# Output bias moved to another place in GpSimd's queue, the maxima transposed ahead of the values, and the fourth head group's products laced into the subtraction

## The reference, cut to what matters

```
x = x + xattn(layernorm(x), ctx, Wq, bq, Wk, bk, Wv, bv, Wo, bo)
        q = (layernorm(x) @ Wq.T + bq) / 4,  k = ctx @ Wk.T + bk,  v = ctx @ Wv.T + bv   (16 heads of 16)
        softmax(q k^T, axis=-1) @ v, heads side by side, then @ Wo.T + bo
x = x + ffn(layernorm(x))
        e = argmax(xf @ router_w.T + router_b)            (32 experts, each token takes one)
        relu(relu(xf @ w1[e] + b1[e]) @ w2[e] + b2[e])
```

## Time and profile before

| what | value |
|---|---|
| median of three runs | 1201.5 us |
| the profiled execution, whole / its span | 1201.21 us / 1199.4 us |
| TensorE busy (matmuls) over the span | 1067.1 us, 89% |
| VectorE busy | 959.8 us, 80% |
| GpSimd busy | 852.9 us, 71% |
| ScalarE busy | 831.7 us, 69% |
| mean granted TensorE clock | 0.970 |
| attention stage | to about 945 us |

### The profile page before, as it was taken

The page is one execution under the profiler, slowest core; times in us unless marked ns, Lnnn a source line. Parts: engine busy times, 40 slices in busy tenths (PEclk is TensorE's granted clock), DMA queues, the critical chain, the costliest instruction groups (busy, mean ns, idle before and its releaser), DMA issues.

```text
span 1199.4 us, 38973 instructions
## 1 busy us (share of the span) xinstructions
PE 1067.1 (89%) x15015; PEld 889.2 (74%) x15015; DVE 959.8 (80%) x2321; ACT 831.7 (69%) x1892; POOL 852.9 (71%) x1613
## 2 busy tenths in 40 slices
PE   6999999899999999999999999999998429989893
PEld 4787777787777777777777777777787329878772
DVE  4878888878888888888888888888888428767762
ACT  4777777677777777777777777777787316656551
POOL 4445777677777777777777777777775747777776
PEclk9999999999999999999999999999999759999997
DMA  7525222522222222222223222222210246666650
GB/s 243 155 57 123 73 73 73 143 73 72 73 73 72 77 78 77 78 73 73 88 73 98 69 84 78 74 73 73 60 38 29 88 129 202 205 205 212 204 161 15
DMA packets 91155, 120.38 MB, mean 100 GB/s; under 512 B 14096, under 2 KB 73883, under 8 KB 90781
## 3 DMA queue, kind: packets, MB, share of 16 engines
q1 hardware_dynamic: 77150, 84.04, 25.0%
q0 software_dynamic: 13824, 33.85, 7.8%
HBM read 60.61 MB, written 59.31 MB: 100 GB/s over the span
## 4 chain that ended last, share of the span: by engine, by line
PE 56%; DVE 26%; DMA 7%; POOL 5%; issue 4%; ACT 1%; SPq 0%; DVEq 0%; POOLq 0%; ACTq 0%
PE pA L763 13%; DVE mx L576 7%; PE sc L817 7%; PE sc L770 6%; DVE nrm L607 6%; PE pA L810 5%; PE sc L792 5%; PE maxima L779 4%; PE sc L754 4%; DVE tr L601 3%; PE sc L997 3%; POOL out L410 3%; DMA arena<-pages 3%; DMA out<-arena 3%; PE maxima L1005 2%
## 5 line engine op out<-in xcount | busy, mean ns | idle before, releaser
L459 ACT ACTIVATE arena<-sc 128x512 f32<-128x512 f32 x512 | 264.5, 604 | 94.8 <-PE sc L801 94.8
L576 DVE TENSOR_REDUCE mx<-maxima 128x4 bf16<-128x512 f32 (+1 forms) x384 | 311.8, 838 | 1.2 <-PE maxima L779 1.2
L410 POOL DMA_INDIRECT out<-arena x160 | 156.8, 980 | 60.9 <-issue 35.4
L379 POOL DMA_INDIRECT pages<-row,slot_i x128 | 132.5, 1035 | 49.8 <-issue 48.6
L817 PE MATMUL sc<-wo_s,aT 128*128 128x256 f32 x512 | 135.0, 386 | 28.9 <-DVE aT L612 26.7
L792 PE MATMUL sc<-qk 32*128 32x256 f32 x2048 | 150.4, 390 | 0.2 <-issue 0.2
L810 PE MATMUL pA<-arena 128*32 128x128 f32 x4096 | 137.9, 275 | 1.1 <-issue 1.1
L607 DVE TENSOR_TENSOR nrm<-tr,inv 128x256 f32<-128x256 f32 x128 | 120.9, 944 | 4.4
L779 PE MATMUL maxima<-qk 32*128 32x128 bf16 x2048 | 103.3, 217 | 23.1 <-DVE mx L576 18.4
L536 ACT ACTIVATE arena<-sc 128x256 f32<-128x256 f32 x160 | 61.3, 383 | 85.4 <-PE sc L988 82.6
L770 PE MATMUL sc<-wqkv,cHi 128*128 128x256 f32 x512 | 120.5, 328 | 0.0
(11 more groups left out here) (138 smaller groups left out, 2607.3 us busy)
## 6 DMA issues: line engine op xcount, KB each, us to landing
arena<-pages SPq DMA_DIRECT2D x160, 130.0 KB
cT<-ctxT SPq DMA_DIRECT2D x64, 256.0 KB, 4.3
xs<-x_in SPq DMA_DIRECT2D x128, 128.0 KB, 3.4
pages<-empty SPq DMA_DIRECT2D x120, 130.0 KB, 3.4
pages<-empty SPq DMA_DIRECT2D x1, 5200.0 KB, 19.7
out<-arena POOLq DMA_INDIRECT x160
w2s<-w SPq DMA_DIRECT2D x1, 2080.0 KB
qk<-w SPq DMA_DIRECT2D x1, 2064.0 KB, 8.4
```

The source lines that it names most:

```text
L379: pool.indirect_dma_start(pages, bass.IndirectOffsetOnAxis(slot_i[:, u:u + 1], 0), row[:, q % 4, u, :], None, bounds_check=last_slot, oob_ ...
L410: pool.indirect_dma_start(out_rows, bass.IndirectOffsetOnAxis(pr[:, r, COL_TOKEN:COL_TOKEN + 1].bitcast(U32), 0), pr[:, r, 0:D], None, bou ...
L459: act.activation(pt[:, u % 2, g].rearrange("p i k -> p (i k)"), sc[g][:, :], ACT.Exp).then_inc(S["exp_out"], 1)
L576: dve.tensor_reduce(mx[:, :].rearrange("p (g h) -> p g h", h=32)[:, g:g + n, 0:4], mball[:, 512 * b:512 * (b + n)].rearrange("p (g h k) -> ...
```

## The change

There are four edits.

1. `add_bo` stands one place further up in GpSimd's pass and a block later: it is `add_bo(s)` right behind `rstd2(s-1, 0)`, and from block 1 on it waits for the `nrm` of unit 2 of the block before.
2. `split` is cut in two. `split_high(s+2)` stays where it was, `rstd2(s-1, 1)` follows it, and `split_low(s+2)` comes behind that.
3. `max_transpose` moves up on TensorE, from behind `values`, logits transpose and ranks to a place between `project_out` and `values`.
4. The fourth group's products stand inside the subtraction. The pairs of groups are now (0, 3) and (1, 2), the exponentials follow in the order 0, 3, 1, 2, and one product of group 3 follows each of the four steps of the second pair. `project_out` waits for the third exponential and `values` for the fourth.

Besides, `stats1` of sequence 0 moves from unit 0 to unit 2. The diff:

```diff
+        EXP_ORDER = (0, 3, 1, 2)
...
                 after(pool, "xn_out", 2, q, 1)
+                if q >= 1:
+                    after(pool, "nrm_out", 4, q - 1, 2)
                 pool.tensor_tensor(xs[:, q % 4], xs[:, q % 4], bo_s[:, :].unsqueeze(1).to_broadcast([P, QB, D]),
...
-            def split(q):
+            def split_high(q):
...
                 pool.tensor_copy(cHi[:, q % 2], cT[:, :, :]).then_inc(S["ctx_hi"], 1)
+
+            def split_low(q):
                 after(pool, "ctx_hi", 1, q, 0)
...
                 if live(s - 1):
                     rstd2(s - 1, 0)
+                if live(s):
+                    add_bo(s)
                 if live(s - 3):
                     place(s - 3)
                 if live(s + 2):
                     rstd1(s + 2)
                 if s >= 0 and live(s + 2):
-                    split(s + 2)
-                if live(s + 1):
-                    add_bo(s + 1)
+                    split_high(s + 2)
+                if live(s - 1):
+                    rstd2(s - 1, 1)
+                if s >= 0 and live(s + 2):
+                    split_low(s + 2)
                 if live(s - 3):
                     slots_as_integers(s - 3)
-                if live(s - 1):
-                    rstd2(s - 1, 1)
-                if live(s - 3):
                     scatter(s - 3)
...
-                        if u == 0:
-                            stats1(s + 3, (0,))
                         if u == 2:
-                            stats1(s + 3, (1, 2))
+                            stats1(s + 3, (0, 1, 2))
...
-            def subtract_max(q, u):
+            def subtract_max(q, u, qn, un):
                 after(pe, "mxT_out", 4, q, u)
-                for pair in ((0, 1), (2, 3)):
+                for pair in (EXP_ORDER[0:2], EXP_ORDER[2:4]):
                     for j in range(4):
                         for g in pair:
...
+                        if pair == EXP_ORDER[2:4] and live(qn):
+                            if j == 0:
+                                after(pe, "max_out", 16, qn, 4 * un)
+                            last_group_for_max(qn, un, j)
...
                     if live(q1):
-                        after(pe, "exp_out", 16, min(s, NQ - 1), 4 * u + 1 if live(s) else 13)
+                        after(pe, "exp_out", 16, min(s, NQ - 1), 4 * u + 2 if live(s) else 14)
                         project_out(q1, u1)
+                    if live(qn):
+                        max_transpose(qn, un)
                     if live(s + 1):
                         if live(s):
-                            after(pe, "exp_out", 16, s, 4 * u + 2)
+                            after(pe, "exp_out", 16, s, 4 * u + 3)
...
                         ranks(s - 2)
-                    if live(qn):
-                        max_transpose(qn, un)
-
```

More of the change, by code:

```diff
@@ L381, in scatter @@
                         bounds_check=last_slot, oob_is_err=False).then_inc(S["scattered"], 16)
-            split(0)
+            split_high(0)
+            split_low(0)
             rstd1(0)
-            split(1)
+            split_high(1)
+            split_low(1)
             for s in range(-1, NQ + 3):
@@ L456, in exps @@
             def exps(q, u):
-                for g in range(4):
-                    after(act, "T_done", 16, q, 4 * u + g)
+                for k, g in enumerate(EXP_ORDER):
+                    after(act, "T_done", 16, q, 4 * u + k)
                     act.activation(pt[:, u % 2, g].rearrange("p i k -> p (i k)"), sc[g][:, :], ACT.Exp).then_inc(S["exp_out"], 1)
@@ L772, in values, with score_for_max, scores_for_max, last_group_for_max @@
                 ins.then_inc(S["V_done"], 1)
-            def scores_for_max(q, u, groups):
-                for j in range(4):
[L776 to L780, removed]
+            def score_for_max(q, u, g, j):
+                m, c = j // 2, j % 2
+                rows = slice(32 * g, 32 * g + 32)
+                return pe.matmul(mb[g % 3][:, j * P:(j + 1) * P], qMh[rows, q % 2, m, c, u * P:(u + 1) * P],
+                                 kTh[rows, q % 2, c, u * P:(u + 1) * P], start=True, stop=True)
+            def scores_for_max(q, u):
+                for j in range(4):
+                    for g in range(3):
+                        ins = score_for_max(q, u, g, j)
                 ins.then_inc(S["S_done"], 1)
+            def last_group_for_max(q, u, j):
+                ins = score_for_max(q, u, 3, j)
+                if j == 3:
+                    ins.then_inc(S["S_done"], 1)
             def max_transpose(q, u):
@@ L872, in _ @@
                             after(pe, "mxT_out", 4, s, u)
-                        scores_for_max(qn, un, (0, 1, 2))
+                        scores_for_max(qn, un)
                     if live(s):
@@ L895, in _ @@
                         scores(s, u)
-                        subtract_max(s, u)
-                    if live(qn):
+                        subtract_max(s, u, qn, un)
+                    elif live(qn):
                         after(pe, "max_out", 16, qn, 4 * un)
-                        scores_for_max(qn, un, (3,))
+                        for j in range(4):
+                            last_group_for_max(qn, un, j)
                     if live(pq):
```

## The result

The changed kernel takes 1164.28 us (median of four runs, 1162.66 to 1166.77), against 1202.39 us before (four runs). The ratio is 0.969, with a 95% interval of 0.966 to 0.972: 3.1% faster. The forecast was 1161 us, the range 1146 to 1185.

A forecast was written before the change was run, and what follows sets the result against it. TensorE was taken as nearly the bound, with VectorE making it wait through `nrm` held by GpSimd's bias. Savings of 37.5, 1.0 and 1.3 us, together 39.8, took 1201.2 to 1161 us; range 1146 to 1185.

The forecast's parts named there:

- The hold and its price: Unit 1's `nrm`, held by GpSimd's `add_bo`: collision and displaced statistics together cost 1.34 us a block (28.76 against 27.42).
- The bias costs nothing in its new place: Behind `rstd2(s-1, 0)` in GpSimd's 2.45 us gap, the bias holds no VectorE operation; cost zero, at most 2 us.
- The split stays behind `nrm`: In unit 1, `nrm` starts 0.4 to 0.5 us before GpSimd's `split_low` and is not held; cost zero.
- The statistics and the transpose: Statistics moved to unit 2: zero; earlier transpose: unit 1's step 7.11 to about 6.80 us, unit 3's 6.94 to 7.10.
- Lacing: Group 3's four products inside the subtraction on TensorE: worth zero, at most 0.13 us a unit.
- The sum: Block 27.26 us against 28.76: 37.5 us over 25 blocks, 1.0 from six others, 1.3 from the first; together 39.8.
- Rival 1: TensorE alone is the bound in the attention stage: block 26.7 us, total 1146 us; chance 0.12.
- Rival 2: TensorE's transpose waits for the maxima in every unit: block 28.06 us, total about 1184 us; chance 0.12.
- Rival 3: The bias collides in its new place, holding `residual` 1.9 us in unit 3: about 1200 us, no change; chance 0.05.
- Rival 4: `split_low` starts first and holds unit 1's `nrm` about 2 us; TensorE waits 0.9 us: 1222 us; chance 0.09.

The follow-up runs named there:

- x1_new_pool: The kernel before with only GpSimd's program taken from the changed kernel (bias ahead of `place`, split cut in two); 1174.38 us, ratio 0.977.
- x9_scan_early: x8_w2_pieces with VectorE's scan of unit 3 moved from behind `xnT_lo` to between the last maxima and `residual`; 1150.95 us, ratio 0.956.
- x2_old_pool: The changed kernel with only GpSimd's program put back to that of before (whole split, then the next block's bias); 1200.03 us, ratio 0.9986.
- x5_stats_only: The kernel before with one edit: the statistics of sequence 0 go from unit 0 to unit 2; 1175.99 us, ratio 0.978.
- x8_w2_pieces: The changed kernel with both 2 MB transfers into `w2s` cut into eight pieces, one a block, weights starting in block 10, not 5; 1153.89 us.
- x7_forced: The changed kernel with `split_low` made to start just ahead of unit 1's `nrm`, behind `split_high` and an unused filler write; 1194.59 us, ratio 0.993.

## Why the prediction was right, and where it was not

**The hold and its price: right.** A block was to go from 28.76 to 27.26 us and went to 27.21. The estimate rested on the one block of the trace before in which `nrm` had come first. x1_new_pool gives the part of the hold by itself: 28.75 - 27.64 = 1.11 us a block, against the 1.13 of 8.24 less 7.11.

**The bias costs nothing in its new place: nearly right.** `residual` and `xnT_lo` were not held. But "none with two SBUF inputs" was wrong: the scan has two. It was held for 0.69 us a block, and 0.11 us of that reached the block: the step out of unit 3 is 7.10 us with the held scan and 6.98 without, both where the scan was moved (x9_scan_early) and where it stayed and the bias had left it (x2_old_pool). I had read the operations by the tensors that they are about, and the scan's second input is a tile of zeros.

**The split stays behind `nrm`: right.** The forecast margin was 0.4 to 0.5 us; `split_low` starts at 507.87, 0.44 us after `nrm` at 507.43.

**The statistics and the transpose: right in sum, less so in the parts.** I took 6.80 for the step out of unit 1 and it is 6.66; I took zero for the statistics in unit 2, and x5_stats_only shows that they cost 0.27 us there (7.03 against 6.76 of the earlier trace rows) unless the transpose comes early; then 0.04. For the wait at the transpose in unit 3 I had 0.17 us on TensorE, and the step came out at 7.10 as forecast, but that was luck: the timeline of TensorE prints no wait at the transpose, probably because `nrm` of that unit is no longer stretched to 0.72 us but takes 0.42. The step is 6.98 us where the scan is free, and the held scan, which I had at nothing, adds the rest.

**Lacing: right at zero.**

**The sum.** 25 blocks at 1.50 gave 37.5 us; the table gives 1.54. Against the forecast of 39.8 us the medians fell by 38.1 and the spans of the two profiled executions by 36.7. In these, 24 of the 25 blocks gained 36.5 us, 0.5 more than forecast. The block with the stop at 109 us became 3.74 us longer. The two around the load of the weights went from 61.54 to 57.72 us, 2.2 us better than the 1.66 in the sum. What follows the last `nrm` of a unit 1, mostly the expert stage, is 1.4 us longer, for which I have no reason; the rest, at most 0.7 us each, nearly cancels. So the total is near the forecast partly by luck: misses of up to 4 us cancel in part. Both large transfers of 2 MB meet the loads of the attention stage, and both excesses vanish in x8_w2_pieces.

**The rivals.** Rival 1 (TensorE alone) fell with lacing's zero. TensorE is printed as busy for 27.10 of 27.22 us, but a matmul's end is modelled; an edit that shortens its own path (lacing) gave nothing and one on VectorE alone (x9_scan_early) gave 0.11 us, so the loop through VectorE still sets the pace, at 27.2 and not at 26.7 us. Rival 2 is excluded by the block of 27.21 us. Rival 3 is seen in the scan alone. Rival 4 was mispriced. I charged 0.9 us for the transpose in front of `values` on top of both waits of the kernel before, 0.91 us for `aT` and 0.51 us in the next unit. In x7_forced TensorE waits 0.35 us for `aT` and 0.52 us at the transpose, and the wait in the next unit is gone: the new wait takes the place of that one. The hold was shorter there, 2.0 us against 2.58, and the full length behind the early transpose was not run. If every further microsecond of hold reached the block, x7_forced's 28.44 us would become 29.0 (0.58 more), and x2_old_pool's 28.49 would become 28.9 (0.33 more, and 0.11 for a held scan). By this estimate the full hold costs at most some 0.2 us over the block before, and not the 0.85 that rival 4 had.

## What to carry to other kernels

When a short two-input operation on VectorE sometimes takes as long as a GpSimd operation beside it, look which of the two starts first, and by how much: here a shift of 0.2 us, from 0.15 us behind to 0.07 us ahead, was worth 26 us. It was won by moving a statistic, by moving the long operation, or by cutting it into four. Cutting is the one of these that doesn't hang on timing. Before moving the long operation into a gap, list every VectorE operation there that reads two SBUF tensors, with constants and zeros counted.

## What the runs showed of the hardware

- A GpSimd operation that reads SBUF and starts first stops a VectorE operation with two SBUF inputs until it ends: 0.43 us became 2.01 to 2.58 (`nrm`), 0.28 became 0.93 (scan), 0.29 became 2.01 (`hot`). It is so with the bias and with the split alike. VectorE starting first costs GpSimd 0.2 us.
- The hold is for one instruction: with four pieces of 0.74 us each the held operation took 0.88 us. The held time is printed as busy.
- VectorE operations with one input in SBUF and one in PSUM were not held beside the bias: 0.42 us (`residual`) and 0.68 us (`xnT_lo`).
- A 2 MB transfer issued once stopped TensorE for 3.64 us with no engine as releaser, and the issue of the load behind it took 4.81 us. In eight pieces, one a block, TensorE had no such stop, and the longest issue of a load in the blocks with a piece of the zeros took 1.8 us.
